# Node numbers of the edge stage's comparisons read from a PSUM bank as float32, edge numbers laid out in pairs

## What is computed

```python
h = (x_flat @ W_gat).reshape(M, HEADS, NUM_EXPERTS)
src = concatenate([edge_index[0], arange(M)])
dst = concatenate([edge_index[1], arange(M)])
e = leaky_relu((h * att_src).sum(-1)[src] + (h * att_dst).sum(-1)[dst], 0.2)
e_max = segment_max(e, dst, M)
ee = exp(e - e_max[dst])
denom = segment_sum(ee, dst, M)
msg = h[src] * (ee / (denom[dst] + 1e-16))[:, :, None]
agg = segment_sum(msg, dst, M)
```

## Time and profile before

| | us |
|---|---|
| three runs, median (lowest to highest) | 2055.55 (2052.54 to 2056.61) |
| the profiled execution: its time | 2052.51 |
| the profiled execution: its span | 2050.7 |
| POOL's first gather of rows starts | 1068.2 |
| DVE's last L1753 starts | 1910.6 |

### The profile page before, as it was taken

How to read it: one execution, slowest core, us unless ns; L and a number is a source line. 1 busy time by engine, 2 the same in 40 slices (tenths; PEclk the granted TensorE clock), 3 DMA queues, 4 the chain that set the end, 5 groups by cost and what they waited for, 6 DMA issues and landing times. The chain is left out here.

```text
span 2050.7 us, 38311 instructions
## 1 busy us (share of the span) xinstructions
PE 938.9 (46%) x13313; PEld 731.9 (36%) x13313; DVE 1410.4 (69%) x2954; ACT 478.6 (23%) x957; POOL 1010.9 (49%) x889
## 2 busy tenths in 40 slices
PE   1223222488888435548963443444434444344200
PEld 1222212366666335532223333343333343334200
DVE  6998999889988488861134655666556665566698
ACT  1222311254554224324431111111111111111110
POOL 0244554466665300000017777777777777777100
PEclk9995555576666557769985555555555555555555
DMA  6000000111111510101000011000000000010000
GB/s 134 10 22 17 24 23 22 39 42 40 42 39 40 126 4 0 41 10 12 0 2 11 11 11 12 10 11 10 12 10 11 10 11 11 11 12 10 4 21 20
DMA packets 113591, 46.59 MB, mean 23 GB/s; under 512 B 92503, under 2 KB 108591, under 8 KB 112802
## 3 DMA queue, kind: packets, MB, share of 16 engines
q0 software_dynamic: 27712, 20.51, 5.6%
q1 hardware_dynamic: 83666, 21.85, 5.6%
q10 hardware_dynamic: 2064, 2.10, 0.5%
HBM read 28.98 MB, written 15.89 MB: 22 GB/s over the span
## 5 line engine op out<-in xcount | busy, mean ns | idle before, releaser
L283 POOL DMA_INDIRECT edges_rows<-table,edges_src x576 | 653.7, 1135 | 178.8 <-issue 175.2
L183 DVE TENSOR_TENSOR sorting_keys<-sorting_keys 128x1024 f32<-128x1024 f32 (+1 forms) x392 | 372.0, 989 | 20.7 <-ACT sorting_keys L264 18.8
L675 POOL DMA_INDIRECT y_rows<-mixture_yt,mixture_xin x143 | 182.8, 1278 | 130.6 <-ACT mixture_yt L890 84.3
L670 POOL DMA_INDIRECT x_rows<-mixture_sent,mixture_slot x128 | 158.8, 1241 | 155.9 <-DVE mixture_slot L732 117.4
L1815 ACT ACTIVATE edges_hotT<-edges_hot_ps 128x1024 bf16<-128x1024 bf16 x74 | 71.7, 1021 | 665.0 <-PE edges_hot_ps L1848 665.0
L1753 DVE TENSOR_TENSOR edges_raw<-edges_rows,edges_side 128x64 f32<-128x64 f32 x36 | 8.0, 221 | 282.6 <-DMA edges_rows<-table,edges_src 282.6
L994 PE MATMUL mixture_bank<-mixture_xT,sorting_w_part 128*128 128x128 bf16 x858 | 118.7, 262 | 48.1 <-DVE mixture_hidden L817 28.6
L1886 PE MATMUL edges_score_bank<-all_ident,edges_score 128*64 128x128 f32 x36 | 14.1, 393 | 261.1 <-DVE edges_score L1755 261.1
L1643 POOL IOTA edges_part_i<- 128x64 int32 x1 | 0.2, 181 | 238.6 <-SPq L1534 238.6
L994 PEld LDWEIGHTS mixture_bank<-mixture_xT,sorting_w_part 128*128 x858 | 86.0, 107 | 83.6 <-issue 74.9
L1342 PE MATMUL convolve_turned<-all_ident,convolve_parts 128*128 128x128 f32 x256 | 51.1, 383 | 113.8 <-DVE convolve_parts L398 113.8
(11 more groups left out here) (379 smaller groups left out, 2557.9 us busy)
## 6 DMA issues: line engine op xcount, KB each, us to landing
edges_rows<-table,edges_src POOLq DMA_INDIRECT x576, 2.4
mixture_xin<-x_rows SPq DMA_DIRECT2D x143, 49.0 KB, 1.8
all_eo<-y_rows SPq DMA_DIRECT2D x16, 256.0 KB, 4.0
y_rows<-mixture_yt,mixture_xin POOLq DMA_INDIRECT x143
sorting_w<-in_L_ffn_w_dram SPq DMA_DIRECT2D x4, 512.0 KB, 8.8
x_rows<-mixture_sent,mixture_slot POOLq DMA_INDIRECT x128, 2.3
out_dram<-all_x_sb SPq DMA_DIRECT2D x8, 256.0 KB
constants_src_i<-in_L_ffn_edge_index_dram SPq DMA_DIRECT2D x1, 1024.0 KB, 4.8
```

The costliest lines, as they stand in the source:

```text
L183: self.st.mark(dve.tensor_tensor(target[half], source[0], source[1], (ALU.min, ALU.max)[half]))
L283: pool.indirect_dma_start(to, None, rows, where).then_inc(done, 16)
L670: pool.indirect_dma_start(x_rows, bass.IndirectOffsetOnAxis(ap=slot[g % 2][:, c, t:t + 1], axis=0), now[c][:, t, :], None).then_inc(scatte ...
L675: pool.indirect_dma_start(y_rows, bass.IndirectOffsetOnAxis(ap=xin[j % XB][:, ROWX - 2:ROWX - 1].bitcast(U32), axis=0), yt[j % YB][:, :], ...
```

## The change

The node numbers are copied once, after the first cast, into a PSUM bank of their own, `node_ps`, as float32 (L1671 of before gets a wait, and a copy of 128x128 follows). All three comparisons read them there. The edge numbers stay in SBUF as bf16, but each is stored twice, side by side, and the comparison walks the node numbers in pairs against such a pair (`equal_to`). So the casts at L1698 to L1700 write 128 in place of 64 elements a partition. To free a bank, the turned scores, which had `score_bank`, lie in columns 128 to 255 of the bank `side`, beside the destination terms. The order of the instructions on every engine is as before but for the one copy that DVE gets ahead of its loop.

```diff
--- before.py
+++ after.py
@@ -1549,11 +1549,11 @@
         src = a.sb("src", [P, T], I32)
         field_t = a.sb("field_t", [P, P], I32)
         local = a.sb("local", [P, T])
-        local16 = a.sb("local16", [P, T], BF16)
+        local16 = a.sb("local16", [P, T, 2], BF16)
         last_n = a.sb("last_n", [P, T], I32)
-        last_n16 = a.sb("last_n16", [P, T], BF16)
+        last_n16 = a.sb("last_n16", [P, T, 2], BF16)
         last_b = a.sb("last_b", [P, T], I32)
-        last_b16 = a.sb("last_b16", [P, T], BF16)
+        last_b16 = a.sb("last_b16", [P, T, 2], BF16)
         field_r = a.sb("field_r", [T, P], I32)
         flags = a.sb("flags", [T, P + 1], BF16)
         rows = a.sb("rows", [P, T, ROW])
@@ -1580,14 +1580,14 @@
         term = a.sb("term", [P, GB * Q])
         term_parts = a.sb("term_parts", [P, 3, GB * Q], BF16)
         hot_ps = [a.ps(f"hot_ps{n}", [P, 512]) for n in range(2)]
+        spread_ps = a.ps("spread_ps", [GC, 512])
         side = a.ps("side", [P, 512])
-        spread_ps = a.ps("spread_ps", [GC, 512])
-        score_bank = a.ps("score_bank", [GC, 512])
         chain = a.ps("chain", [P, 512])
         keys_ps = a.ps("keys_ps", [P, 512])
         times_ps = a.ps("times_ps", [P, 512])
+        node_ps = a.ps("node_ps", [P, 512])
         ad_ps, seen_ps = side[:, 0:GC], side[:, GC:GC + GB]
-        score_ps = score_bank[:, 0:P]
+        score_ps = side[0:GC, P:2 * P]
         end_ps, found_ps, now_ps = (chain[:, n * GC:(n + 1) * GC] for n in range(3))
         sum_ps = chain[:, 3 * GC:3 * GC + GB * Q]
         numbered = a.sem("numbered")
@@ -1668,7 +1668,8 @@
             dve.sem_inc(at_ready, 1)
             dve.wait_ge(numbered, 2)
             st.mark(dve.tensor_copy(block_f[:, :], part_i[:, :]))
-            st.mark(dve.tensor_copy(node16[:, :], node_i[:, :]))
+            st.link(dve.tensor_copy(node16[:, :], node_i[:, :]))
+            st.mark(dve.tensor_copy(node_ps[:, 0:P], node16[:, :]))
             st.mark(dve.tensor_copy(ident16[:, :], ident[:, :]))
             st.mark(dve.memset(one16[:, :], 1.0))
             st.mark(dve.memset(zero16[:, :], 0.0))
@@ -1695,9 +1696,9 @@
                 st.mark(dve.tensor_tensor(local[:, :], field_t[:, 0:T], block_f[:, :], ALU.subtract))
                 st.mark(dve.tensor_scalar(last_n[:, :], field_t[:, T:2 * T], P - 1, None, ALU.bitwise_and))
                 st.link(dve.tensor_scalar(last_b[:, :], field_t[:, T:2 * T], 7, None, ALU.logical_shift_right))
-                st.mark(dve.tensor_scalar(local16[:, :], local[:, :], 255.0, None, ALU.min))
-                st.mark(dve.tensor_copy(last_n16[:, :], last_n[:, :]))
-                st.link(dve.tensor_scalar(last_b16[:, :], last_b[:, :], float(T), 255.0, ALU.subtract, ALU.min))
+                st.mark(dve.tensor_scalar(local16[:, :, :], per_channel(local[:, :], 2), 255.0, None, ALU.min))
+                st.mark(dve.tensor_copy(last_n16[:, :, :], per_channel(last_n[:, :], 2)))
+                st.link(dve.tensor_scalar(last_b16[:, :, :], per_channel(last_b[:, :], 2), float(T), 255.0, ALU.subtract, ALU.min))
 
             def place_flags(st):
 
@@ -1714,15 +1715,20 @@
                 st.link(dve.tensor_scalar(starts.at_f[:, :], starts.at_f[:, :], float(E), None, ALU.min))
                 dve.tensor_copy(at_i[:, :], starts.at_f[:, :]).then_inc(at_ready, 1)
 
+            def equal_to(to, numbers, n, which):
+
+
+                return dve.tensor_tensor(to[:, :, :].rearrange("p t (n two) -> p t n two", two=2),
+                                         numbers[:, 0:n].rearrange("p (n two) -> p n two", two=2).unsqueeze(1)
+                                         .to_broadcast([P, GB, n // 2, 2]),
+                                         which.unsqueeze(2).to_broadcast([P, GB, n // 2, 2]), ALU.is_equal)
+
             def one_hot(g):
-                dve.tensor_tensor(hot[g][:, :, :], node16[:, :].unsqueeze(1).to_broadcast([P, GB, P]),
-                                  per_channel(local16[:, tiles(g)], P), ALU.is_equal).then_inc(hot_ready, 1)
+                equal_to(hot[g], node_ps, P, local16[:, tiles(g), :]).then_inc(hot_ready, 1)
 
             def one_hot_last(st, g):
-                st.mark(dve.tensor_tensor(hot_last[g % 2][:, :, :], node16[:, :].unsqueeze(1).to_broadcast([P, GB, P]),
-                                          per_channel(last_n16[:, tiles(g)], P), ALU.is_equal))
-                dve.tensor_tensor(hot_block[g % 2][:, :, :], node16[:, 0:T].unsqueeze(1).to_broadcast([P, GB, T]),
-                                  per_channel(last_b16[:, tiles(g)], T), ALU.is_equal).then_inc(last_ready, 1)
+                st.mark(equal_to(hot_last[g % 2], node_ps, P, last_n16[:, tiles(g), :]))
+                equal_to(hot_block[g % 2], node_ps, T, last_b16[:, tiles(g), :]).then_inc(last_ready, 1)
 
             dve.wait_ge(keys_turned, 1)
             place_sources(st, slice(0, LAST * GB), src_ready[0])
```

## The result

| | us |
|---|---|
| before, median of 4 runs (lowest to highest) | 2055.93 (2052.54 to 2056.61) |
| the change, median of 4 runs | 1949.01 (1947.18 to 1951.29) |
| ratio, 95% interval | 0.9484 (0.9467 to 0.9500) |
| predicted: time (range) | 1957.6 (1942 to 1976) |
| profiled execution of the change: time, span | 1947.18, 1945.4 |

A forecast was written before the change was run, and what follows sets the result against it. The prediction took POOL's issue of gathers to bound the edge stage. Its terms, -110.0 + 11.5 + 0.3 + 0.3 = -97.9 us, took the median from 2055.5 to 1957.6 us, range 1942 to 1976.

The forecast's parts named there:

- The bound: Edge stage: POOL's stream of gathers paces it, 23.4 us a group, where undisturbed gathers would need 20.3 us.
- The long holds: Edge stage: 72 gathers, one in each L1718 and L1722, are no longer held by these comparisons, -110.0 us.
- Rival 1: Comparisons L1718 and L1722: they still hold the gathers, so no change, 2056 us; chance 0.05.
- the seven pairs with L753: Trace rows: stores beside L753, which has one PSUM and one SBUF input, were none stretched; one took 0.96 us.
- Smaller holds: Edge stage: shorter DVE instructions with two SBUF inputs, and casts, now hold gathers, +11.5 us, bounds 0 and 27.
- The comparisons' own length: L1718, L1722 and L1724: +7 ns from a PSUM input, hidden except in the last group, +0.02 us.
- The higher fixed cost: Three comparisons: PSUM sources pay 120 cycles instead of 58, an estimated 65 ns each, 0.2 us in the last group.
- Rival 2: Three comparisons: new pattern slows them; DVE bounds from factor 1.8; chance 0.03 still faster than before, 0.03 slower.
- Rival 3: Three comparisons: pairs let them run two elements a cycle, 2.9 us less in the last group, 1954.7 us; chance 0.05.
- The copy and its wait: Before DVE's loop: copying node numbers into PSUM and waiting behind the first cast, +0.3 us, bounds 0 and +0.6.
- The last turn's casts: Three casts widened to 128x128 once a turn: hidden by idle time except in the last turn, +0.3 us.
- The side bank: Turned scores: PE writes the same transpose to another address, its waits unchanged, 0 us.

## Why the prediction held

*The bound.* POOL's gathers pace the stage on the chips where before takes 2056 us. The edge stage of four kernels, from the first gather to the last L1753, L1759, L1760 or L1763, less the gathers' sum:

| kernel | stage | gathers' sum | difference |
|---|---|---|---|
| before | 842.4 | 653.7 | 188.8 |
| the change | 739.4 | 550.7 | 188.8 |
| float32 in SBUF, chip 3 | 847.1 | 658.3 | 188.8 |
| bf16 pairs in PSUM, chip 3 | 742.8 | 554.1 | 188.7 |

Each microsecond off a gather came off the stage, within 0.1 us (the differences are taken before rounding).

*The long holds,* -110.0 us: right, in size and in cause. All 72 are gone with the PSUM input, and all 72 are back with the same instruction on SBUF. Rival 1, that the hold stays, fell, as the seven pairs with L753 had said. By the Trainium skill (SBUF — State Buffer, "Who interferes with whom") an instruction with two SBUF inputs takes the shared read interface, and that agrees: held with two (2.70 us for a gather in L1722), not with one (0.94 in L1721). The page says it of a GpSimd instruction that reads SBUF, and the gather is one: it takes its row numbers from `edges_src`. By its inferred addition, that tensor_tensor spares descriptor generation, nothing would have been freed, and 110 us were. That does not refute the addition, though: a gather that begins only 0.03 us ahead of such an instruction is not held at all, so what is held may be no more than its first step, such as the reading of the row numbers. No run separates the two.

*Smaller holds,* +11.5 us: the one term that was mis-sized. Measured: 550.66 - 543.74 = 6.9 us. The four instructions of 0.49 us gave 6.1, against 7.9 in the estimate: 23 gathers in L1636 with 1.19 us each make 5.7 of that, one in L1638 and three in L1798 the rest. The three casts gave nothing against 1.9, the short ones 0.8 against 1.8. The estimate spread the gathers' starts evenly over the instructions. They are not even: DVE's group starts when the rows land, so each instruction meets the gathers in the same place of their 1.25 us, group after group. In 23 groups a gather began with 0.37 to 0.39 us of L1636 to go; 21 began 0.03 to 0.04 us ahead of L1801 and passed. A mean over phases is no price where the phases are locked. The bounds of 0 and 27 did hold. One reading behind the term was wrong too: a gather need not have "got through its first 0.12 us" before the instruction starts, as those 21 show. The 0.12 lies at the other end, as said of the counts above, and there the formula has it right.

*The comparisons' own length:* right. 2283, 2282 and 1212 ns against 2281, 2283 and 1217. The higher fixed cost that the Trainium skill gives for PSUM (VectorE: DVE Perf Modes, "The TRN2 errata"), 65 ns each as an estimate from it, isn't there: 2, -1 and -5 ns. Rival 2 fell with it. (Its factor of 1.7 for L2005 is 1.6 against the trace's straight reduction of 2048 elements, L1120 with 2286 ns; nothing hung on it.) Rival 3 fell too, for the reason given against it: float32 on one side. The pairs do double the rate when both sides are bf16 (1218 ns in SBUF, 1217 in PSUM), and that rival's price, 2.9 us in the last group and nothing else, was near: behind the last L1763 the kernel with bf16 in PSUM takes 2.0 us less than the change, and its stage is no shorter.

*The copy and its wait,* +0.3 us: from the start of the first gather of keys to that of the first rows it takes 4.50 us in before, 4.85 now, so +0.35, ahead of the stage. *The last turn's casts,* +0.3: the three last 258, 228 and 220 ns against 234, 201 and 193, so 0.08 us a turn. *The side bank,* 0: nothing in the table above is left for it.

*The sum:* -97.9 predicted, -106.9 measured. With the measured terms it is -110.0 + 6.9 + 0.35 + 0.1 = -102.6. The first two lie in the stage, which gave -103.0. The earlier start of 2.5 us makes most of the way from there to the profiled executions' difference of 105.3, and the 1.6 from there to the medians' is within the spread of four runs (4 us from lowest to highest); neither belongs to a term of the sum. So of the 9.0 us between forecast and result some 4.6 are the smaller holds' size, and most of the rest is spread that happened to point the same way. What was to be seen was seen: L1759 every 20.5 us ((1805.1 - 1086.7) / 35; 20.6 predicted), its waits 176.2 (175), the gathers' sum 550.7 (555), none over 1.4 us.

*What the prediction never considered* is that the kernel's bound depends on the chip. "POOL paces the stage" was read from one trace and holds for its chip; where PE stalls, the same change came out at 1.0144, of which, with 1% between two runs of one kernel there, the absence of a gain is the safe part.

## What to carry to other kernels

Look for indirect gathers or stores, issued by GpSimd, whose duration is a multiple of the median, and for the VectorE instruction that they began in: if it has two SBUF inputs, move one into PSUM, best a constant one, which costs a single copy. Check first, on the chip it will run on, that GpSimd's stream is what the others wait for. Count such delays by phase, from the timeline of a group, not as an average.

## What the runs showed of the hardware

- A GpSimd indirect DMA that begins while a VectorE instruction with two SBUF inputs is at work ends 0.82 us after that instruction, whether it lasts 2.28, 1.22, 0.68 or 0.49 us; with one of the inputs in PSUM it takes its 0.94 us.
- The order of the starts decides. 21 gathers that began 0.03 to 0.04 us ahead of L1801 took their 0.94 us, and so did those that began up to 0.04 us into an instruction with two SBUF inputs. Then it is the VectorE instruction that grows: in before, L1638 of the run ends and maxima (128x64) takes 0.28 to 0.29 us in the five groups where a gather begins 0.02 to 0.04 us into it, and 0.22 to 0.23 in the 67 others. The same in the first run with PSUM and no pairs, from its timeline:

```profile
1328.96 0.30 DVE L1638 TENSOR_TENSOR edges_left<-edges_left,edges_end_parts 128x64 f32<-128x64 f32 x1
1329.00 0.95 POOL L283 DMA_INDIRECT edges_rows<-table,edges_src  x1 [0.31 <-issue]
```

- A cast can hold one too: in the kernel with bf16 in PSUM, 17 gathers that began 0.22 us before the end of the cast L1640 (SBUF float32 to bf16) took 1.03 us on average, each to 0.81 or 0.82 us after its end.
- A comparison with bf16 numbers in PSUM and bf16 pairs in SBUF takes 1217 ns for 2048 elements and 680 ns for 1024, as with both in SBUF (1218 and 684). With float32 in PSUM it is 2283 for 2048.
- One program takes 2056 us on one chip and 2430 to 2437 on three others, each time steady within 8 us over 9 to 19 runs. In the edge stage PE there stands still for its own issue, up to 13 us at a time.
